# Dealing the head's work lists of a sparse attention and expert block to the engines in another order

## The reference

```python
xn = _layernorm(x)
out = x + attn(xn) + ffn(xn)
# attn: second layer norm with ln_g, ln_b; q, k, v and gate projections;
#       k = k * sigmoid(gate); q, k = elu(q) + 1, elu(k) + 1;
#       causal linear attention: (tril(q k^T) v) / (sum(q * cumsum(k)) + 1e-6)
# ffn:  scores = (xn @ router_w^T + router_b) / temperature
#       three Sinkhorn rounds, the two best of 8 experts for each token,
#       xn + sum over the two of gate * ((relu(xn wg) * (xn wp)) wo)
```

## Time and profile before

| | us |
|---|---|
| three timed executions | 359.4, 359.29, 358.01 (median 359.29) |
| profiled execution, its own time | 357.82 |
| its span from the first to the last instruction | 356.1 |

### The profile page before, as it was taken

How to read it: one execution, slowest core, us unless ns; L and a number is a source line. 1 busy time by engine, 2 the same in 40 slices (tenths; PEclk the granted TensorE clock), 3 DMA queues, 4 the chain that set the end, 5 groups by cost and what they waited for, 6 DMA issues and landing times.

```text
span 356.1 us, 8790 instructions
## 1 busy us (share of the span) xinstructions
PE 331.0 (93%) x2560; PEld 302.5 (85%) x2560; DVE 265.4 (75%) x745; ACT 233.2 (65%) x431; POOL 266.9 (75%) x385
## 2 busy tenths in 40 slices
PE   0899889889999999997999999999999999999992
PEld 0599659567888888886999999999989999999992
DVE  3889689998988988887667676677656767676661
ACT  2589653323767767675877775777777777777650
POOL 5569999975777776657677777767767777777776
PEclk9999999987999999999999999999999999999998
DMA  6999999998244333358599987526665556574110
GB/s 186 302 336 333 336 333 302 312 281 249 93 155 150 121 135 108 112 152 253 164 296 375 356 260 243 182 91 196 195 176 164 149 166 167 145 224 123 48 48 16
DMA packets 63763, 71.50 MB, mean 201 GB/s; under 512 B 5768, under 2 KB 58390, under 8 KB 63718
## 3 DMA queue, kind: packets, MB, share of 16 engines
q1 hardware_dynamic: 54016, 48.70, 49.5%
q0 software_dynamic: 8672, 21.98, 17.1%
q10 hardware_dynamic: 1030, 0.27, 0.4%
HBM read 28.28 MB, written 43.04 MB: 200 GB/s over the span
## 4 chain that ended last, share of the span: by engine, by line
PE 73%; POOL 11%; DVE 9%; issue 3%; ACT 3%; DMA 1%; ACTq 0%; DVEq 0%; POOLq 0%
PE psum L1834 18%; PE psum L1819 9%; PE psum L1820 8%; PE psum L1821 8%; POOL rows L579 6%; PE psum L1716 4%; PE psum L1698 4%; PE psum L1809 3%; PE psum L1634 3%; POOL rows L516 3%; PE psum L1600 2%; PE psum L1606 2%; PE psum L1557 2%; PE psum L1559 2%; PE psum L1561 2%
## 5 line engine op out<-in xcount | busy, mean ns | idle before, releaser
L635 POOL DMA_INDIRECT out<-rows x70 | 68.8, 983 | 22.8 <-issue 14.9
L617 POOL DMA_INDIRECT by_lower<-rows,slot_u x64 | 63.7, 996 | 26.6 <-issue 14.9
L1819 PE MATMUL psum<-xT_high,w_now 128*128 128x256 f32 x256 | 77.1, 301 | 1.9 <-DVE xT_low L1413 1.1
L851 ACT ACTIVATE w_now<-w_split 128x1024 fp32r x63 | 66.7, 1059 | 15.0 <-PE psum L1821 14.7
L1834 PE MATMUL psum<-w_expert,hT 128*128 x560 | 75.5, 276 | 1.0 <-DVE hT L1422 0.7
L1820 PE MATMUL psum<-xT_low,w_now 128*128 128x256 f32 x256 | 72.0, 281 | 0.0
L1821 PE MATMUL psum<-xT_high,w_now 128*128 128x256 f32 x256 | 71.9, 281 | 0.0
L1834 PEld LDWEIGHTS psum<-w_expert,hT 128*128 128x128 f32 x560 | 68.8, 191 | 1.7 <-issue 1.5
L626 POOL DMA_INDIRECT by_upper<-rows,goes_to x58 | 56.2, 969 | 18.7 <-issue 10.1
L1426 DVE TENSOR_TENSOR hT<-relu,psum 128x512 f32<-128x512 f32 x64 | 44.0, 687 | 34.2 <-PE psum L1821 16.7
L870 ACT ACTIVATE relu<-psum 128x512 f32<-128x512 f32 x64 | 38.2, 597 | 22.8 <-PE psum L1821 22.4
(11 more groups left out here) (282 smaller groups left out, 667.8 us busy)
## 6 DMA issues: line engine op xcount, KB each, us to landing
by_lower<-blank SPq DMA_DIRECT2D x1, 10140.0 KB, 35.2
by_upper<-blank SPq DMA_DIRECT2D x1, 10062.0 KB, 70.3
rows<-by_upper SPq DMA_DIRECT2D x32, 258.0 KB, 3.1
rows<-by_lower SPq DMA_DIRECT2D x26, 260.0 KB, 4.8
rows<-in_L_attn_x SPq DMA_DIRECT2D x8, 512.0 KB, 7.4
lead_row<-by_lower SPq DMA_DIRECT2D x6, 260.0 KB, 4.0
out<-rows POOLq DMA_INDIRECT x70, 2.4
w_expert<-in_L_ffn_wg SPq DMA_DIRECT2D x8, 128.0 KB, 3.0
```

The lines of the kernel that those rows point to most:

```text
L617: pool.indirect_dma_start(by_lower, bass.IndirectOffsetOnAxis(ap=slot_u[:, t:t + 1], axis=0), rows[:, t, :], None)\
L635: pool.indirect_dma_start(out_rows, bass.IndirectOffsetOnAxis(ap=row(n)[:, k, TOKEN:TOKEN + 1].bitcast(U32), axis=0), row(n)[:, k, BASE], ...
L851: act.activation(w_now[:, n % 2, :], w_split[:, bass.ds(number, 1), 0:4 * FF].rearrange("p a f -> p (a f)"), ACT.Copy).then_inc(w_copied, 1)
L1819: pe.matmul(target, high, x_high, start=True, stop=False)
```

## The change

Only the order and the distribution of the head's work change; no computation is added or left out. The statistics, roots, scales and sums are the same operations as before.

- Variances: block 1 goes to GpSimd and blocks 3 and 4 to VectorE, so GpSimd has blocks 1 and 2, VectorE 0, 3 and 4.
- Normalising: ScalarE has groups 1, 3, 7 (four groups before), VectorE 5, 10, 13, 14 (four before), GpSimd the other nine (eight before).
- Emptying PSUM: all 16 `save_zT` and all 16 `save_lv` are ScalarE's; VectorE had three and two.
- TensorE: the router weights' transpose comes first of all; group 1 is turned ahead of group 0; logits of groups 1 and 2 are issued ahead of the rest sum, which before stood ahead of the turns of groups 3 and 2.
- The orders `TURN_ORDER` and `LV_ORDER` and the call order on each engine are new. VectorE's routing waits for the same groups as before, in three parts.

```diff
--- before.py
+++ after.py
@@ -309,12 +309,13 @@
 
         BLOCKS = [(0, C), (C, 2 * C)] + [(t0, t0 + 2 * C) for t0 in range(2 * C, NT, 2 * C)]
         block_of = {t // G: k for k, block in enumerate(BLOCKS) for t in range(*block)}
-        DVE_BLOCKS = 2
-        ACT_Z, DVE_Z, POOL_Z = (1, 3, 5, 9), (4, 11, 12, 15), (0, 2, 6, 7, 8, 10, 14, 13)
-        ACT_ZT, DVE_ZT = (0, 1, 3, 2, 6, 4, 7, 9, 11, 10, 14, 15, 13), (5, 8, 12)
-        ACT_LV, DVE_LV = (1, 0, 2, 3, 6, 5, 7, 8, 11, 9, 10, 13, 15, 14), (4, 12)
-        TURN_ORDER = (0, 1, 3, 2, 6, 5, 4, 7, 8, 9, 11, 10, 14, 15, 13, 12)
-        LV_ORDER = (1, 0, 2, 3, 6, 4, 5, 7, 8, 11, 9, 10, 13, 15, 12, 14)
+        POOL_BLOCKS = (1, 2)
+        DVE_BLOCKS = (0, 3, 4)
+        ACT_Z, DVE_Z, POOL_Z = (1, 3, 7), (5, 10, 13, 14), (0, 2, 6, 4, 11, 8, 9, 12, 15)
+        ACT_ZT, DVE_ZT = (1, 0, 2, 3, 6, 7, 5, 4, 10, 11, 9, 8, 13, 12, 14, 15), ()
+        ACT_LV, DVE_LV = (1, 2, 3, 6, 5, 10, 0, 11, 4, 7, 9, 12, 14, 8, 15, 13), ()
+        TURN_ORDER = (1, 0, 2, 3, 7, 6, 5, 4, 10, 11, 9, 8, 13, 12, 14, 15)
+        LV_ORDER = (1, 2, 3, 6, 5, 10, 0, 11, 4, 7, 9, 12, 14, 8, 15, 13)
         TURN_BANKS = tuple(TURN_ORDER[at::3] for at in range(3))
         LV_BANKS = tuple(LV_ORDER[at::2] for at in range(2))
         turn_bank = {g: 4 + at for at, line in enumerate(TURN_BANKS) for g in line}
@@ -519,7 +520,7 @@
 
             def variances_by_four(k):
                 ts = slice(*BLOCKS[k])
-                at = 4 * (k - DVE_BLOCKS)
+                at = 4 * POOL_BLOCKS.index(k)
                 pool.wait_ge(batch_done, BLOCKS[k][1] // C)
                 pool.tensor_tensor(m_dif[:, ts], stats[:, ts, 1], stats[:, ts, 4], ALU.subtract).then_inc(var_step, 1)
                 pool.tensor_tensor(m_sum[:, ts, :], stats[:, ts, 1:3], stats[:, ts, 4:6], ALU.add).then_inc(var_step, 1)
@@ -529,22 +530,22 @@
                 pool.wait_ge(var_step, at + 4)
                 pool.tensor_tensor(var[:, ts], var[:, ts], m_dif2[:, ts], ALU.add).then_inc(var_pool, 1)
 
+            variances_by_four(1)
             normalise(0)
+            normalise(2)
+            variances_by_four(2)
             pool.wait_ge(rw_step, 2)
             pool.tensor_scalar(rbt[:], rb[:], rtemp[:], None, ALU.mult).then_inc(rbt_ready, 1)
-            normalise(2)
-            variances_by_four(2)
             normalise(6)
-            variances_by_four(3)
-            normalise(7)
+            normalise(4)
+            normalise(11)
             normalise(8)
-            variances_by_four(4)
-            normalise(10)
-            normalise(14)
-            normalise(13)
+            normalise(9)
             pool.wait_ge(w_step, 1)
             pool.tensor_scalar(w_in[:, WK], w_in[:, WK], 0.5, None, ALU.mult).then_inc(w_step, 1)
             pool.tensor_scalar(w_in[:, WQ], w_in[:, WQ], 1.0 / P, None, ALU.add).then_inc(w_step, 1)
+            normalise(12)
+            normalise(15)
 
             for k in range(PACK):
                 pool.memset(powers[:, k:k + 1], float(E ** k)).then_inc(pack_ready, 1)
@@ -658,11 +659,11 @@
 
             def root(k):
                 t0, t1 = BLOCKS[k]
-                if k < DVE_BLOCKS:
-                    act.wait_ge(var_dve, k + 1)
+                if k in DVE_BLOCKS:
+                    act.wait_ge(var_dve, DVE_BLOCKS.index(k) + 1)
                     share_of = 1.0
                 else:
-                    act.wait_ge(var_pool, k - DVE_BLOCKS + 1)
+                    act.wait_ge(var_pool, POOL_BLOCKS.index(k) + 1)
                     share_of = 0.25
                 act.activation(sq[:, 0, t0:t1], var[:, t0:t1], ACT.Sqrt, bias=eps[:, 0:1], scale=share_of)
                 act.activation(sq[:, 1, t0:t1], var[:, t0:t1], ACT.Sqrt, bias=eps[:, 1:2], scale=share_of * (1.0 + LN_EPS))\
@@ -685,41 +686,45 @@
                                ACT.Copy).then_inc(lv_act, 1)
 
             root(0)
+            normalise(1)
             root(1)
-            normalise(1)
+            save_zT(1)
             normalise(3)
             save_zT(0)
-            save_zT(1)
+            save_zT(2)
+            root(2)
             save_zT(3)
-            root(2)
-            save_zT(2)
+            normalise(7)
             save_lv(1)
-            save_lv(0)
-            normalise(5)
             save_lv(2)
+            root(3)
             save_zT(6)
-            root(3)
-            save_zT(4)
+            save_zT(7)
+            save_zT(5)
             save_lv(3)
             save_lv(6)
-            save_zT(7)
-            normalise(9)
+            save_zT(4)
+            save_zT(10)
             save_lv(5)
+            save_zT(11)
+            save_lv(10)
             root(4)
+            save_lv(0)
+            save_lv(11)
+            save_zT(9)
+            save_zT(8)
+            save_lv(4)
             save_lv(7)
-            save_zT(9)
-            save_zT(11)
+            save_zT(13)
+            save_zT(12)
+            save_lv(9)
+            save_zT(14)
+            save_zT(15)
+            save_lv(12)
+            save_lv(14)
             save_lv(8)
-            save_zT(10)
-            save_zT(14)
-            save_lv(11)
-            save_lv(9)
-            save_zT(15)
-            save_zT(13)
-            save_lv(10)
+            save_lv(15)
             save_lv(13)
-            save_lv(15)
-            save_lv(14)
 
             def tanh_gate(n):
                 act.wait_ge(g_ready, n + 1)
@@ -1174,40 +1179,34 @@
             block_variances(0)
             batch_stats(1)
             block_scales(0)
-            block_variances(1)
             router_temperature()
             router_weights()
             value_weights()
+            batch_stats(2)
             block_scales(1)
-            batch_stats(2)
             batch_stats(3)
             centre_router()
             batch_stats(4)
             block_scales(2)
             batch_stats(5)
-            normalise(4)
+            block_variances(3)
+            normalise(5)
+            block_scales(3)
+            normalise(10)
             batch_stats(6)
-            save_zT(5)
-            block_scales(3)
             batch_stats(7)
-            save_lv(4)
-            normalise(11)
-            save_zT(8)
+            block_variances(4)
+            rest_weights()
             block_scales(4)
-            normalise(12)
+            normalise(13)
             stat_link(dve.tensor_tensor(root2[:], sq[:, 1, :], rs[:, 0, :], ALU.mult))
-            rest_weights()
-            normalise(15)
+            normalise(14)
             dve.wait_ge(rbt_ready, 1)
-            dve.wait_ge(lv_act, max(ACT_LV.index(g) for g in range(NG // 2) if g in ACT_LV) + 1)
-            dve.wait_ge(lv_dve, DVE_LV.index(4) + 1)
+            dve.wait_ge(lv_act, max(ACT_LV.index(g) for g in range(NG // 2)) + 1)
             shift_rows(0, B // 2)
-            save_zT(12)
-            dve.wait_ge(lv_act, ACT_LV.index(10) + 1)
+            dve.wait_ge(lv_act, max(ACT_LV.index(g) for g in range(NG // 2, NG - GB * 2)) + 1)
             shift_rows(B // 2, B - 2)
-            save_lv(12)
             dve.wait_ge(lv_act, len(ACT_LV))
-            dve.wait_ge(lv_dve, len(DVE_LV))
             shift_rows(B - 2, B)
             gate_key(0)
             spread_maxima()
@@ -1501,50 +1500,50 @@
                                      zT[:, g * G + t, :], w_lv[:], start=True, stop=True)
                 last.then_inc(lv_ready[g], 1)
 
+            pe.wait_ge(rw_loaded, 16 * 3)
+            pe.transpose(psum[:, 3, 0:E], rw_raw[:], ident[0:E, 0:E]).then_inc(rw_pe, 1)
             pe.wait_ge(spread_ready, 2)
             pe.matmul(psum[:, 1, 0:D], share[:], bias_in[:, WV], start=True, stop=False)
             pe.matmul(psum[:, 1, 0:D], spread[:], w_raw[:, WV], start=False, stop=True).then_inc(w_summed, 1)
-            pe.wait_ge(rw_loaded, 16 * 3)
-            pe.transpose(psum[:, 3, 0:E], rw_raw[:], ident[0:E, 0:E]).then_inc(rw_pe, 1)
             pe.wait_ge(rw_step, 3)
             pe.matmul(psum[:, 2, 0:E], minus[:], rw_turned[:], start=True, stop=True).then_inc(rw_pe, 1)
+            turn_z(1)
             turn_z(0)
-            turn_z(1)
+            turn_z(2)
+            turn_z(3)
+            pe.wait_ge(rw_step, 5)
+            pe.wait_ge(w_lv_ready, 1)
+            logits_values(1)
+            logits_values(2)
             pe.wait_ge(w_loaded, 16 * 4)
             pe.matmul(psum[:, 7, REST], share[:], bias_in[:, REST], start=True, stop=False)
             pe.matmul(psum[:, 7, REST], spread[:], w_raw[:, REST], start=False, stop=True).then_inc(w_summed, 1)
-            turn_z(3)
-            turn_z(2)
-            pe.wait_ge(rw_step, 5)
-            pe.wait_ge(w_lv_ready, 1)
-            logits_values(1)
+            turn_z(7)
+            turn_z(6)
+            logits_values(3)
+            turn_z(5)
+            logits_values(6)
+            turn_z(4)
+            turn_z(10)
+            logits_values(5)
+            turn_z(11)
+            logits_values(10)
```

(29 more changed lines are left out.)

## The result

The changed kernel takes 358.97 us (median of 20 executions, 357.25 to 361.11); the kernel before, executed beside it, 358.10. Two executions of the kernel before are recorded at 637.57 us, 278 us above all its others; the ratio, taken over fast executions alone, leaves them out. It is **1.0030, 95% interval 1.0018 to 1.0042**: 1.1 us slower, 0.6 to 1.5 (the medians differ by 0.9). The forecast was +0.8 us, "the same". The forecast number 360.1 sits 1.1 us above the measured one, almost all of it because the three executions shown before had a median 1.2 us above that of the twenty. The profiled execution took 358.76 us, 0.94 more than the 357.82 of before.

A forecast was written before the change was run, and what follows sets the result against it. The prediction took TensorE to bound the head: -0.4 + 1.5 + 0.2 - 0.5 = +0.8 us at the last emptying, passed on one to one, gave 360.1 us, "the same"; range 357.9 to 362.2, the likeliest's own 359.0 to 361.6.

The forecast's parts named there:

- The bound: Head, 0 to 41 us: TensorE bounds it, busy 21.78 of 21.85 us from the first logits on.
- The opening: Head's start: value sum waits behind the temperature's DMA, block 1's scales come 2.6 us later, first logits at 17.8, -0.4 us.
- The rest sum: TensorE's full stretch: the sum now stands behind logits(2) at full clock, +1.5 us, bounds 1.3 and 3.0.
- The clock's part and the waits: TensorE's full stretch: starting 0.4 earlier at half clock costs +0.2 us; fewer waits give -0.5, bounds 0 and -1.0.
- ScalarE, VectorE, GpSimd: Head: ScalarE's +1.2 us is hidden by TensorE, VectorE's slack grows, GpSimd's base loop starts some 0.8 earlier for nothing.
- the second softmax part: VectorE: 1.7 us of work beginning about 1.9 us before the last logits are out, just fitting; 0 to +0.5.
- Sum: Last emptying of PSUM: +0.8 us, 41.6 instead of 40.8, passed on one to one to the whole time.
- Rival 1 (later clock): Head: TensorE's gap at 14.2 to 16.1 us delays the full clock, +2.5 us, 361.8; chance 0.25.
- Rival 2 (the slow stretch goes): 77.40 to 84.20 us: the stretch at clock 0.50 vanishes, -3.4 + 0.8 = -2.6 us, 356.7; chance 0.10.
- the missing stretch near 77 us: Sign of being wrong: the stretch at granted clock 0.50 near 77 us is absent from the changed profile.
- Rival 3 (GpSimd): GpSimd's base loop sets the end, so its 0.8 us earlier start is the gain: 358.5; chance 0.10.
- Rival 4 (an earlier landing, no waits): Head: the temperature's DMA lands earlier, logits start at once and all waits go: +0.3, 359.6; chance 0.08.

The follow-up runs named there:

- experiment 5: The changed kernel with the rest sum's matmuls issued a second time at their place; ratio to the kernel before 1.0039 (1.0020 to 1.0057).
- (9): The kernel before with 44 small bf16 matmuls ahead of TensorE's value sum and 4 behind each router piece; ratio to the kernel before 0.9951.
- (8): The changed kernel with 46 small bf16 matmuls ahead of TensorE's first piece and 20 behind the turns of groups 1 and 0; ratio to the kernel before 0.9937.
- Experiment 1: The changed kernel with the value weight sum back ahead of the router weights' transpose; ratio to the kernel before 0.9997 (0.9979 to 1.0015).
- experiment 4: The kernel before with only the router weights' transpose moved ahead of the value weight sum; ratio to the kernel before 1.0015 (1.0000 to 1.0030).
- experiment 3: The kernel before with only the rest sum moved behind the first two groups of logits; ratio to the kernel before 0.9956 (0.9934 to 0.9979).

## Why the prediction was right, point by point

- **The bound.** Right: TensorE 23.23 of 23.27 us from the first logits on; experiment 5 lengthens the stretch by its full 1.56 us; with nothing added but small matmuls the head ends 2.5 us sooner in (9) and 1.8 in (8).
- **The opening.** value_weights at 11.81 (forecast 12.0), block 1's variance on GpSimd 1.29 us (1.39 taken from a row twice as wide), its reciprocal at 13.63 (13.85), TensorE's gap 2.25 us (1.9), turn of group 2 at 15.97 (16.1), first logits at 17.73 (17.8). Experiment 1 undoes the loss, clear of its interval; in experiment 4 the reordered start alone costs 0.78 us at the head's end, in the average 0 to 1.1.
- **The rest sum.** +1.5 forecast, 1.58 in place. Right as a size; the simple sum hid that the old place wasn't free at half clock, though: its 3.0 us held back the logits by 2.4 us (experiment 3). The prediction counted this only as "-0.4 at the start", which is what the late opening left of it.
- **The clock's part and the waits.** The stretch from the first logits to the end of the last emptying grew from 22.58 to 23.89, 1.31 us, where 1.5 + 0.2 - 0.5 = +1.2 was forecast. Of the 1.31 the rest sum is 1.58; the lower level covers 1.80 us of the stretch instead of 1.13, of which half, 0.33, is lost, against 0.2 forecast. That leaves -0.6 for the waits, an estimate as a remainder, against -0.5, a term for which the prediction doesn't show its stepping.
- **ScalarE, VectorE, GpSimd.** All hidden, as forecast; the second softmax part did not quite fit (0.17 us).
- **Sum.** Head +0.79 against +0.8; profiled execution +0.94, the average +1.1 (0.6 to 1.5). The mechanism held, term by term; that the terms' errors of 0.1 each cancel to 0.01 is luck, and so is the draw. With this opening the DMA landed between 8.82 and 10.56 in four profiles, and the clock rose between 18.37 and 19.90.
- **Rival 1 (later clock).** Not in this profile: the clock rises at 19.53 us, against 19.38 before. It can come later, at 21.22 in experiment 1, where the first sixteen instructions of the logits took 0.93 us more.
- **Rival 2 (the slow stretch goes).** It went and another came. The prediction named the missing stretch near 77 us as a sign of being wrong; the sign came and the rival did not, since the stretches come and go: 38 of 91 executions of the kernel before have none. Its price of 3.4 us was mis-sized: measured 0.6 to 2.4. VectorE's own pace would explain that: it is busy 6.54 of 6.80 us in that stretch and 6.52 at full clock in the changed kernel. This is argued from two rows, not tested.
- **Rival 3 (GpSimd).** Wrong: 0.94 us earlier, all of it idle again.
- **Rival 4 (an earlier landing, no waits).** The DMA landed at 10.10, 0.16 us sooner than in the earlier trace rows, which gave little: +0.79 at the head's end and not +0.3.

## What to carry to other kernels

A list of work dealt anew is worth what it does on the engine that is full; more slack on VectorE and an earlier base loop on GpSimd bought nothing here. In an in-order queue, look at what the first instruction waits for before putting it first: the transpose waits for the temperature's DMA, which it doesn't read, and the sum behind it holds up VectorE's value_weights and all that follows there. (A wait for the router weights alone wasn't tried.) And where a short head runs on TensorE, see its clock first: small matmuls in its waits gave 3.3 us, three times what the reordering lost.

## What the hardware showed that I had not expected

- The page's clock row prints 9 from the start, yet the same weight loads take 331 ns and later 190 ns. The trace's clock record only begins with the rise, at 19.4 us; before it, the pace of the instructions is the witness.
- The clock did not rise with TensorE's being busy: from 11.62 to 19.4 us it was busy almost throughout, with transposes and two sums whose moving part is 384 columns wide, one of them with one row only the earlier trace rows. 44 to 46 small bf16 matmuls in a row brought the rise to 8.1 to 10.2 us in five kernels. In one of them, (8), it fell again at 11.88.
The Trainium skill, "TensorE: Matmul & The Clock Gate", section "What's actually happening", has the throttled level as the default and activity as what lifts it. By that rule the early stretch should have lifted it; these rows don't show it doing so before 19.4 us, and here the measurement decides.
- The landing of the three small router DMAs varies: the waiting transpose started at 8.82, 10.10, 10.33 and 10.56 us in four executions. The kernel before isn't free of it either: VectorE's router pieces stand ahead of value_weights and wait for the same landing, 1.07 us in experiment 1. What the new opening adds is VectorE's wait of 1.20 us for the sum behind the transpose.
